# A fused S4 and LSTM kernel on one core: own memory for the second unit's rows, another order of the first unit, and a finer table of preparation steps

## What is computed

```
x = x + layernorm(gelu(long_convolution(layernorm(x))))      # kernel of the convolution from B, C, P, Q, Lam
x = x + layernorm(ffn(layernorm(x)))

ffn:  ft = sigmoid(xt @ wf.T + c @ uf.T + bf)
      it = sigmoid(xt @ wi.T + c @ ui.T + bi)
      gt = tanh   (xt @ wc.T + c @ uc.T + bc)
      c  = ft * c + it * gt                    # scanned over 8 steps, the batches here
      h  = tanh(xt @ wo.T + c_final @ uo.T + bo)
```

## Time and profile before

| | |
|---|---|
| median of 3 runs | 2726.28 us |
| profiled execution | 2723.82 us |
| its span, first to last instruction | 2722.0 us |
| TensorE busy | 2581.3 us, 95% |
| VectorE busy | 1908.0 us, 70% |
| ScalarE busy | 1527.5 us, 56% |
| GpSimd busy | 949.4 us, 35% |
| mean granted TensorE clock | 0.976 |

### The profile page before, as it was taken

The page is one execution under the profiler, slowest core; times in us unless marked ns, Lnnn a source line. Parts: engine busy times, 40 slices in busy tenths (PEclk is TensorE's granted clock), DMA queues, the critical chain, the costliest instruction groups (busy, mean ns, idle before and its releaser), DMA issues.

```text
span 2722.0 us, 54926 instructions
## 1 busy us (share of the span) xinstructions
PE 2581.3 (95%) x21507; PEld 2098.1 (77%) x21507; DVE 1908.0 (70%) x3404; ACT 1527.5 (56%) x2844; POOL 949.4 (35%) x1449
## 2 busy tenths in 40 slices
PE   4499999986899999999998899999999999999998
PEld 4278888875788888888887788888888888644443
DVE  7855655557876777677767777676777674578778
ACT  6666767565655555555556555555555553345444
POOL 7778677722121212121221221221212220145444
PEclk9799999998999999999998899999999999999999
DMA  9879778887564554444545644543555443378777
GB/s 327 297 236 323 272 260 305 290 302 242 124 152 98 116 126 128 98 111 121 134 102 139 168 105 114 126 128 94 117 119 134 97 110 97 126 276 303 259 258 263
DMA packets 524549, 489.95 MB, mean 180 GB/s; under 512 B 275584, under 2 KB 406912, under 8 KB 519040
## 3 DMA queue, kind: packets, MB, share of 16 engines
q1 hardware_dynamic: 524288, 486.43, 60.5%
HBM read 270.60 MB, written 150.73 MB: 155 GB/s over the span
## 4 chain that ended last, share of the span: by engine, by line
PE 85%; DVE 5%; ACT 3%; DMA 3%; issue 2%; POOL 1%; SPq 0%; DVEq 0%; POOLq 0%; ACTq 0%
PE bank L1926 28%; PE bank L1936 28%; PE bank L1994 12%; PE bank L1815 4%; PE bank L1765 3%; PE bank L1823 3%; PE bank L1801 3%; PE bank L1777 2%; PE bank L1978 2%; DMA big<-yd 1%; DMA big<-xr 1%; DVE big L1360 1%; PE bank L1785 1%; ACT big L1153 1%; DMA big<-big 0%
## 5 line engine op out<-in xcount | busy, mean ns | idle before, releaser
L1926 PE MATMUL bank<-big 128*128 128x256 f16 x8064 | 1098.0, 276 | 47.0 <-ACT big L1181 18.0
L1936 PE MATMUL bank<-big 128*128 128x256 f16 x7056 | 963.3, 273 | 0.0
L1926 PEld LDWEIGHTS bank<-big 128*128 128x128 f16 x8064 | 797.1, 99 | 156.5 <-ACT big L1181 21.1
L1936 PEld LDWEIGHTS bank<-big 128*128 128x128 f16 x7056 | 690.8, 98 | 80.2
L893 POOL TENSOR_SCALAR big<-big 128x1 f32<-128x1 f32 x256 | 55.6, 217 | 1277.0 <-DVE big L1472 753.8
L1994 PE MATMUL bank<-big 128*128 128x512 f16 x1536 | 332.2, 379 | 0.0
L1153 ACT ACTIVATE big<-big 128x512 f32<-128x512 f32 x384 | 290.9, 805 | 61.1 <-DVE big L1642 60.7
L1994 PEld LDWEIGHTS bank<-big 128*128 128x128 f16 x1536 | 150.3, 98 | 181.3
L1642 DVE TENSOR_TENSOR big<-bank,big 128x512 f32<-128x512 f32 x192 | 131.3, 684 | 222.9 <-PE bank L1936 215.4
L1188 ACT ACTIVATE big<-bank 128x512 f32<-128x512 f32 x192 | 113.9, 593 | 263.5 <-PE bank L1936 253.4
L1066 ACT ACTIVATE big<-big 128x512 f32<-128x512 f32 x256 | 206.5, 807 | 93.3 <-POOL big L895 92.7
(11 more groups left out here) (210 smaller groups left out, 3573.2 us busy)
## 6 DMA issues: line engine op xcount, KB each, us to landing
big<-xr SPq DMA_DIRECT2D x16, 2048.0 KB, 11.1
big<-xg SPq DMA_DIRECT2D x64, 512.0 KB, 7.8
big<-kpad SPq DMA_DIRECT2D x32, 1024.0 KB, 12.2
yd<-big SPq DMA_DIRECT2D x16, 2048.0 KB, 16.9
big<-x SPq DMA_DIRECT2D x128, 256.0 KB, 3.3
x1d<-big SPq DMA_DIRECT2D x128, 256.0 KB, 2.0
xtd<-big SPq DMA_DIRECT2D x64, 512.0 KB, 4.8
big<-xtd SPq DMA_DIRECT2D x64, 512.0 KB, 4.2
```

Source lines behind the costliest of these rows:

```text
L1926: ins = e.matmul(o, WX[2 * g + lw][:, q, kt, 128 * a:128 * a + 128], slot[u % 2][:, part, lx, k0 + kt, :], start=(first and kt == 0 and (l ...
L1936: ins = e.matmul(o, WC[2 * g + lw][:, q, kt, 128 * a:128 * a + 128], cc[unit(u)[1] % 2][:, qc, lx, kt, :], start=False, stop=end, skip_gro ...
```

## The change

The same work is done, with the same operations. What changes is memory, order and waits:

- Unit 1's rows of yd get memory of their own (`y1t`, at `y0_at`). Loads for unit 1 wait for less, and unit 2's rows are loaded during unit 1's preparation. Since a buffer of states shares that memory, the first `state_high` also waits for the preparation of unit 1 (ss at 16, xlo at 16).
- For unit 0, the four parts made of plain rows come ahead of the four made of sums (`item`), on all engines. TensorE's first two products wait for four parts (xlo at 4), the third for eight.
- SyncE: two of the six loads of input weights (WX 4 and 5) come behind the stores of yd and the loads for unit 1; the loads of state weights are spread over unit 1's stores; the store of what was turned for unit 0 comes behind.
- TensorE's order in a group is now 4, 1, then 3 of the group before, 2, 5, then 7 of the group before, 6. ScalarE copies ka ahead of k5, and the gate functions and the cell update of group n-2 (not n-1) are done at the start of round n. The product of two gates is written to zt[2] instead of zt[1].
- The preparation of a unit is no longer a table of six stages but of 18 steps for VectorE and 16 for ScalarE, each with its group and place (four places for VectorE, three for ScalarE). Units 1 to 4 and 16 to 18 have rows of their own.

```diff
+STEADY = {
+    "dve": ((0, 0), (0, 0), (0, 0), (1, 0), (1, 0), (1, 2), (2, 0), (2, 2), (2, 2), (3, 0), (3, 2), (4, 0), (4, 0), (4, 2), (4, 2), (4, 2), (5, 2), (5, 2)),
+    "act": ((0, 2), (0, 2), (1, 0), (1, 2), (2, 0), (2, 1), (2, 1), (2, 2), (3, 0), (3, 2), (3, 2), (4, 0), (4, 1), (4, 2), (5, 2), (5, 2)),
+}
+SPECIAL = {
+    1: {"dve": ((0, 0), (0, 0), (0, 0), (1, 0), (1, 0), (1, 2), (2, 0), (2, 2), (2, 2), (3, 0), (3, 2), (4, 0), (4, 0), (4, 2), (4, 2), (4, 2), (4, 2), (4, 2)),
+        "act": ((0, 2), (0, 2), (1, 0), (1, 2), (2, 0), (2, 1), (2, 1), (2, 2), (3, 0), (3, 2), (3, 2), (4, 0), (4, 1), (4, 2), (4, 2), (4, 2))},
...
+    16: {"dve": ((87, 0), (87, 0), (87, 0), (87, 2), (87, 2), (88, 0), (88, 0), (88, 2), (88, 2), (88, 2), (89, 0), (89, 2), (89, 2), (89, 2), (91, 2), (91, 2), (92, 2), (92, 2)),
+        "act": ((87, 1), (87, 1), (87, 2), (88, 0), (88, 0), (88, 1), (88, 1), (88, 2), (89, 0), (89, 1), (89, 1), (89, 2), (91, 1), (91, 2), (92, 1), (92, 1))},
+    17: {"dve": ((94, 0), (94, 0), (94, 0), (95, 0), (95, 0), (95, 2), (96, 0), (96, 0), (96, 0), (96, 2), (97, 0), (97, 0), (97, 0), (97, 2), (97, 2), (97, 2), (98, 0), (98, 0)),
+        "act": ((94, 2), (94, 2), (95, 0), (95, 2), (96, 0), (96, 0), (96, 0), (96, 1), (96, 2), (97, 0), (97, 0), (97, 1), (97, 2), (97, 2), (98, 1), (98, 1))},
+    18: {"dve": ((99, 0), (99, 0), (99, 0), (99, 2), (99, 2), (100, 0), (100, 0), (100, 2), (100, 2), (100, 2), (101, 0), (101, 2), (101, 2), (101, 2), (103, 2), (103, 2), (104, 2), (104, 2)),
+        "act": ((99, 1), (99, 1), (99, 2), (100, 0), (100, 0), (100, 1), (100, 1), (100, 2), (101, 0), (101, 1), (101, 1), (101, 2), (103, 1), (103, 2), (104, 1), (104, 1))},
+}
+def prep_schedule(engine):
+
+    at = {(g, place): [] for g in range(GROUPS + 6) for place in range(4)}
     for v in range(1, NU):
-        if v <= 4:
-            places = ((0, 1, 2, 3, 4, 4), (5, 6, 7, 8, 9, 10), (11, 12, 13, 14, 15, 15), (16, 17, 18, 19, 20, 20))[v - 1]
-        else:
-            places = [6 * v - 9 + r for r in range(6)]
-        for stage, g in enumerate(places):
-            at[g].append((stage + 1, v))
+        for step, (g, place) in enumerate(STEADY[engine]):
+            if v in SPECIAL:
+                g, place = SPECIAL[v][engine][step]
+            else:
+                g += 6 * v - 9
+            at[g, place].append((step, v))
     return at
-PREP_AT = prep_schedule()
+DVE_AT, ACT_AT = prep_schedule("dve"), prep_schedule("act")
...
+        y1t = f32(y0_at, 2048).rearrange("p (g k h) -> p g k h", g=NG, k=4)
         xb = [f32(m0_at + 2048 + 512 * c, 512) for c in range(4)]
         xs16 = [f16(x0_at + 512 * k, 512).rearrange("p (l h) -> p l h", l=2) for k in range(4)]
...
+            if e < 8:
+
+                e = (0, 1, 4, 5, 2, 3, 6, 7)[e]
             return e // 8, e % 8 // 4, e % 4
+
+        def rows_y(v):
+
 
         def source(e):
 
             v, p, k = item(e)
             if v == 0:
...
                 w.wait_ge(s["y1"], 16 * 8)
-                w.wait_ge(s["x1"], 4 * v)
-                if v > 1:
+                if v == 1:
+                    w.wait_ge(s["yc"], 2)
+                elif v == 2:
+
+                    w.wait_ge(s["x1"], 4)
+                    w.wait_ge(s["yl"], 32)
+                else:
                     w.wait_ge(s["ss"], 8 * v)
                     w.wait_ge(s["xh"], 8 * v - 2)
                     w.wait_ge(s["xlo"], 8 * v - 2)
-                e.dma_start(yt, src).then_inc(s["yl"], 16)
+                e.dma_start(rows_y(v), src).then_inc(s["yl"], 16)
 
             def load_x1(v, c):
                 b, j = unit(v)
...
-                    for k in range(4, 8):
-                        turn(8 * v + k)
-                    if v + 1 < NU:
-                        load_x1(v + 1, 1)
-                        load_x1(v + 1, 3)
-                    store_xt(v)
+            def prepare(v):
+                for r in range(4):
+                    store_x1(v, r)
+                    if v == 1 and r == 1:
+                        load_y(2)
+                    if v == 1 and r:
+                        load_WC(r + 2)
+                if v == 1:
+                    store_xt(0)
+                for k in range(4):
+                    turn(8 * v + k)
+                if v + 1 < NU:
+                    load_x1(v + 1, 0)
+                    load_x1(v + 1, 2)
+                if 1 < v < NU - 1:
+                    load_y(v + 1)
+                for k in range(4, 8):
+                    turn(8 * v + k)
+                if v + 1 < NU:
+                    load_x1(v + 1, 1)
+                    load_x1(v + 1, 3)
+                store_xt(v)
 
 
             w.wait_ge(s["cv"], G * (NG - 1))
@@ -650,8 +686,6 @@
             e.dma_start(fbs, accd.rearrange("g p h -> p g h")).then_inc(s["accs"], 16)
             for c in CHUNKS[2:]:
                 load_x1(0, c)
-            load_WX(4)
-            load_WX(5)
             store_y(NG - 2)
             store_y(NG - 1)
             w.wait_ge(s["cv"], G * NG)
@@ -660,21 +694,23 @@
             load_y(1)
             for c in CHUNKS:
                 load_x1(1, c)
+            w.wait_ge(s["wx"], 16 * 4)
+            load_WX(4)
+            load_WX(5)
             w.wait_ge(s["w_lo"], low_base(8))
             w.wait_ge(s["wd"], stored(7))
+            w.wait_ge(s["fb"], 12)
+            load_WC(0)
+            load_WC(1)
 
             w.wait_ge(s["fb"], 20)
-            for n in range(6):
-                load_WC(n)
-            store_xt(0)
-
-            for n in range(GROUPS):
-                for stage, v in PREP_AT[n]:
-                    prepare(stage, v)
+            load_WC(2)
+            for v in range(1, NU):
+                prepare(v)
 
                 for j in range(2):
                     last = unit_at(j, 7)
-                    if n == 6 * last + 8:
+                    if v == last + 2:
                         w.wait_ge(s["chi"], state_parts(last))
                         w.wait_ge(s["clo"], state_parts(last))
                         e.dma_start(cfd[j], cc[j][:, 0:4].rearrange("p q l a t -> p (q l a t)")).then_inc(s[f"cfd{j}"], 16)
...
+                if step < 4:
+                    norm1(n + step)
+                elif step in (4, 5, 8, 11):
+                    norm2(n + (4, 5, 8, 11).index(step))
+                else:
+                    high(i + (6, 7, 9, 10, 12, 13, 14, 15).index(step))
@@ -1130,6 +1129,9 @@
                 if place == 0:
                     w.wait_ge(s["cn"], 2 * u + 2)
                     w.wait_ge(s["p7"], 6 * u + 6)
+
+                    w.wait_ge(s["ss"], 16)
+                    w.wait_ge(s["xlo"], 16)
                     if j >= 2:
                         w.wait_ge(s[f"cfd{j % 2}"], 16)
                     e.activation(c16[:, 0:2, 0], c32[:, 0:2], ACT.Copy).then_inc(s["chi"], 1)
 
             for n in range(4):
                 norm1(n)
-            for n in range(4):
-                norm2(n)
-            for i in range(8):
+            norm2(0)
+            norm2(1)
+            high(0)
+            high(1)
+            norm2(2)
+            norm2(3)
+            for i in range(2, 8):
                 high(i)
@@ -1170,28 +1176,28 @@
 
                     w.wait_ge(s["p6"], n)
                     e.activation(zt[(n - 1) % 3][:, 1, :], bank_a(n - 1)[:, 0:256], ACT.Copy).then_inc(s["k6"], 1)
-                if u and gi == 1:
+                if 2 <= n <= GROUPS + 1:
+                    gates(n - 2)
+                if u and gi == 2:
                     state_high(u - 1, 0)
-                for stage, v in PREP_AT[n]:
-                    prepare(0, stage, v)
+                for step, v in ACT_AT[n, 0]:
+                    prepare(step, v)
                 if n < GROUPS:
 
-                    w.wait_ge(s["pb"], n + 1)
-                    w.wait_ge(s[("fc", "cn", "ig")[n % 3]], n // 3)
-                    e.activation(zt[n % 3][:, 3, :], bank_b(n)[:, 256:512], ACT.Copy).then_inc(s["k5"], 1)
-                if u and gi == 1:
-                    state_high(u - 1, 1)
-                for stage, v in PREP_AT[n]:
-                    prepare(1, stage, v)
-                if n < GROUPS:
                     w.wait_ge(s["pa"], n + 1)
+                    w.wait_ge(s[("fc", "ig", "cn")[n % 3]], n // 3)
                     e.activation(zt[n % 3][:, 0::2, :], bank_a(n)[:, :].rearrange("p (q t) -> p q t", q=2), ACT.Copy).then_inc(s["ka"], 1)
                 if u and gi == 2:
+                    state_high(u - 1, 1)
+                for step, v in ACT_AT[n, 1]:
+                    prepare(step, v)
+                if n < GROUPS:
+                    w.wait_ge(s["pb"], n + 1)
+                    e.activation(zt[n % 3][:, 3, :], bank_b(n)[:, 256:512], ACT.Copy).then_inc(s["k5"], 1)
+                if u and gi == 3:
                     state_high(u - 1, 2)
-                for stage, v in PREP_AT[n]:
-                    prepare(2, stage, v)
-                if 1 <= n <= GROUPS:
```

(63 more changed lines are left out.)

134 lines of the change are left out of this document (25 added, 109 removed).

## The result

The changed kernel takes 2700.57 us, the median of 4 runs (2699.39 to 2701.77); the kernel before takes 2727.22 us beside it (4 runs, 2723.93 to 2733.60). The ratio is 0.990, with a 95% interval of 0.9881 to 0.9918: 26.7 us faster, by the medians. The forecast was 2692 us in a range of 2672 to 2713 us.

The account below looks back on a forecast made before the run. TensorE bounds the recurrence, with some 70 us lost where ScalarE's copies come late behind VectorE, at the start and units 15 and 17. Gains 11.8 + 18.3 + 1.5 = 31.6 us from 2723.8 give 2692 us, range 2672 to 2713 us.

Parts of the forecast that it names:

- the signs named: Right: among others, under 7 us lost in each transition; wrong: among others, TensorE waiting for ka in units with state.
- The start: Groups 0 to 11: earlier rows and removed waits gain 2.8 + 3.2 + 2.9 + 2.9 = 11.8 us, between 4 and 20.
- The wait for x1d: At the start, VectorE's first sum of rows waits for the store of x1; 3.2 us less.
- the one for SyncE's queue: At the start: fourth store issued at about 637 us, last transpose for group 6 at about 651 us, in time for TensorE.
- The transitions: Units 15 and 17: the finer table takes preparation off VectorE, gaining 18.3 us, at least 8 and at most 30.
- the better case: Rival that almost everything goes: start gives 17 us, transitions 27 us, through a chain relaxed by one round; 2678 us, chance 0.15.
- The DMA wait of 3.6 us: At unit 17 VectorE waits 3.6 us for rows; the new table asks for them earlier, taking the load off the path.
- bunching and clock: Losses left in units 15 and 17: waits of 3.9 and 5.1 us from bunched steps, plus 1.5 us each for low clock.
- Units with state: The new order gives k5 and k6 more room, gaining 1.5 us; the longer ka chain is costed at nothing.
- the slower rival: In units with state, ka's chain in every third group is longer than reckoned, by VectorE's backlog; 2770 us, chance 0.05.
- Bunching: Rival: steps stay dense around the transitions and k6 bounds the start; each part gives 8 us, about 2708 us, chance 0.2.
- Of clock, 3.0 us: Transitions: 1.5 us kept for each unit; if short waits keep full clock, 2689 us instead of 2692 us.

Follow-up runs that it names:

- u_table: The changed kernel without its own table rows for units 16 to 18, which follow the steady row: 2703.58 us.
- f_gates: The changed kernel with VectorE's cell update ahead of the first preparation steps in every third round with state: 2697.30 us.
- f_turns: The changed kernel with unit 1's first four transposes right behind the stores of x1, three state-weight loads and unit 0's store behind everything of unit 1: 2698.06 us.

## Why the prediction was right, and where not

**The frame was right.** What bounds the kernel, where its 70 us are lost, and that nothing but the recurrence would move, came out: the head takes 382.4 us in both executions, and units with state from group 111 on run at 9.17 us a group. Sum 31.6 us, measured 23.6 us from the last gelu in the profiled executions and 26.7 us by the medians. Of the signs named, two came out against it: TensorE waits for ka in units with state (groups 16, 22 and 100), and the transition at unit 17 lost 7.5 us and not under 7.

**The start, 11.8 us forecast, 9.1 us measured** (10.2 and 11.2 us in the two other executions with the same program up to group 12; of before there is one)**.** VectorE's first statistics came at 619.02 us, which is 617.5 us when the later end of the convolution is taken off, as forecast. The wait for x1d fell from 3.2 to 0.6 us and the wait for rows to 0.8 us. The step that failed is the one for SyncE's queue. The fourth store was issued at 636.95 us, as reckoned, and no product of group 6 waited for a transpose. But I had looked only for who waits at group 6 and overlooked ScalarE's high in group 4, which reuses the buffer that the first transpose reads, and I had no price for an issue that holds SyncE. The trace of before had one to show, right behind a load of rows:

```profile
652.71 0.38 SPq L583 DMA_DIRECT2D big<-yd  x1
653.13 4.77 SPq L609 DMA_TRANSPOSE big<-big  x1
```

Unit 0's order, which I had counted at nothing of its own, is worth some 2 to 4 us.

**The transitions, 18.3 us forecast, 17.8 us measured, for a reason that is only a third right.** The sum of work on VectorE by groups was my whole argument, and the own table rows of units 16 to 18, which it priced, are worth 6.0 us there, 4.0 us with what they cost in groups 99 to 101. The step that failed is that I gave the delay of the gates no term in the sum, only a place in the better case: taken out of the changed kernel it costs 21 us, and the transitions lose 34.0 us instead of 12.9. It needs rows that are asked for earlier, without which it gave nothing. The DMA wait of 3.6 us was named and counted; that ScalarE's norm1 stands for the same rows was not:

```profile
1454.93 0.81 ACT L1066 ACTIVATE big<-big 128x512 f32<-128x512 f32 x1 [4.94 <-POOL big L895]
```

The waits of cell updates for gate functions stood in the view of groups as 74.5 us of idle time ahead of L1611 (43.3 us ahead of L1596 in the changed kernel), and I read only its duration. That the sum hit is chance: I priced the work that leaves at 8.7 us a transition and left the rest to bunching and clock, and the errors cancel. One size is off too: of unit 15's 15.3 us I took 10.6 us as waits, and TensorE's waits in that stretch add up to 9.8 us.

**Units with state, 1.5 us gained forecast, 3.3 us lost measured** (7.6 us of new waits, for 4.3 us of old ones at groups 12, 13, 22 and at the end)**.** The chain that I described for the slower rival is the one that bites: ka waiting for the product of two gates in every third group. In 53 of 56 such groups it costs nothing or under 0.3 us, as I took it; in groups 16, 22 and 100 it costs 3.8, 1.9 and 2.0 us. The step that failed is that I priced the chain with VectorE's work alone and not with a wait inside it: at group 16 the statistics ahead of the product stand 3.7 us for rows, at group 22 3.3 us. At group 100 they don't wait; there VectorE is late by its own work. A wait at 809.51 us, which I had expected to go, is the same weak place in the old order.

**The rivals.** Bunching (2708 us) was nearer in mechanism than in time: the transitions kept 13 us where I had left 12. The slower case did not come, since the chain has its 2.7 us of air nearly everywhere. Of clock, 3.0 us were kept for two transitions; in the first block on the result the clock there is 0.96, which over 42 and 45 us is about 1.7 us lost in each, 3.4 us. In unit 15 TensorE stood 2.29 us ahead of the product at 1436.46 us, and then the granted clock was 0.50, the level of 1.2 GHz, for 3.4 us (stretch, length and busy times as in the first block):

```profile
1437.80:1441.20 3.40, 3.40 (x19) 2.40 (x17) 3.33 (x7) 0.18 (x1) 0.00 (x0) 0.50 1.03 118
```

By what the prediction took from the Trainium skill (TensorE: Matmul & The Clock Gate, "HAM oscillation"), short waits would have cost no clock at all. The trace shows no such line: in the transitions the clock fell for a short while, where the longest waits are 2.3 us, and in the stretch from 700 to 1419 us it is 1.00, with a wait of 3.60 us in it.

## What to carry to other kernels

When an engine is short of time in one stretch, list what it waits for there before moving work away, and who else stands for the same data. Here the round of delay gave nothing alone; with the rows a group earlier the transitions lost 5 us less of 31 us, and with the rest of the change 18 us less. In a queue worked in order, a wait for data that stands ahead of an urgent step lends its whole length to that step, so put the step that others wait for first and the one that waits for a DMA behind it. When loads are moved from one place of a DMA queue to another, follow every later issue of that queue to the engine that waits for it, and not only the loads themselves.

## What the runs showed of the hardware

The issue of a DMA can hold SyncE far longer than its neighbours. In the recurrence of the kernel before, 31 DMAs are issued next behind a load of rows of yd. Thirty of them are transposes, and they took 4.09 to 5.42 us to issue; the other, a load of x, took 1.71 us. No other DMA there took over 2.23 us, and most transposes took 1.2 to 1.5 us. In the changed kernel it is a weight load of 896 KB that comes right behind such a load, and it took 6.89 us (6.47 and 6.08 us in u_table and f_gates), against 0.4 to 0.8 us for the others.

The first two transposes of unit 1 took 4.5 and 4.1 us, with some 4 MB of loads and stores issued and not landed; the rows of yd had landed by then. In f_turns, where these loads come later, they took 1.4 and 1.3 us. It isn't the bytes alone: the kernel before has six weight loads and two stores outstanding at 621.9 us, over 6 MB, and issued all of them in 0.4 to 0.7 us each. Whether the small pieces of the rows of yd are the reason was not tried.

The convolution ended up to 10 us apart, though no experiment touches its work: the last gelu began at 595.3 to 597.9 us in 13 executions and at 605.0 us in one. That one was late from the start: its first gelu came at 151.1 us, where the others had 141.4 to 143.9 us. Effects of 2 or 3 us had to be read from the stretches behind it, since few runs of the whole time don't resolve them.
